# TensorE's main loop: one block per turn instead of two, its head placed on a fetch-block boundary

## The reference, cut to what matters

```python
xn = layernorm(x)
# branch 1: a state-space layer, chunked
z, xs, B, C, dt = split(xn @ in_proj_w)              # 1024, 1024, 64, 64, 16 columns
xs = silu(causal_conv1d(xs, conv_w, conv_b))         # 4 taps
B, C = elu(B) + 1, elu(C) + 1
a = exp(-softplus(dt + dt_bias) * exp(A_log))
y = ssd_chunked(C, B, xs, a) + D * xs                # 16 heads of 64, state 64 x 64
y = rmsnorm(y) * norm_scale * silu(z)
out1 = y @ out_proj_w
# branch 2: a gated feed-forward layer, with Hadamard transforms around its weights
u = hadamard(xn * SU_ug)
h = silu(u @ W_gate.T * s_gate) * (u @ W_up.T * s_up)
out2 = hadamard(h * SU_dp) @ W_down.T * s_down
return x + out1 + out2
```

## Time and profile before

| | |
|---|---|
| time, median of 3 runs | 1880.8 us (1873.93 to 1884.12) |
| profiled execution: span from first to last instruction | 1883.3 us |
| profiled execution: time around the span | not given; its span lies inside the range of the three times |
| PE busy | 1808.6 us, 96% of the span |
| PE weight loads | 1244.5 us, 66% |
| DVE, ACT, POOL busy | 74%, 65%, 16% |
| chain that ended last | PE 80%, DVE 10%, "issue" 3% |
| instruction fetches on queue q8 | 129 packets, 2.11 MB |

### The profile page before, as it was taken

One profiled execution on the slowest core, in us unless ns is written; L12 is line 12 of the kernel. 1 busy time (PEld: TensorE's weight loads), 2 busy tenths in 40 slices (PEclk: granted clock), 3 DMA queues, 4 the chain that ended last, 5 costly groups with the idle time before them and its releaser, 6 DMA issues.

```text
span 1883.3 us, 40159 instructions
## 1 busy us (share of the span) xinstructions
PE 1808.6 (96%) x13745; PEld 1244.5 (66%) x13746; DVE 1387.9 (74%) x2859; ACT 1228.6 (65%) x2583; POOL 308.9 (16%) x270
## 2 busy tenths in 40 slices
PE   5779999999999999999999999999999999999998
PEld 2346767576776767576766768677675757666674
DVE  6986867768585877758585877858686786848686
ACT  7957848476665848566574848556583857658483
POOL 0000202112030202103030211203020211203020
PEclk9989999999999999999999999999999999999999
DMA  8212122221312222121312222121312312131222
GB/s 320 71 65 57 47 57 80 46 71 34 79 43 75 62 57 79 32 71 44 81 46 58 79 46 74 37 72 46 88 49 57 79 32 82 34 80 46 61 75 57
DMA packets 217544, 125.60 MB, mean 67 GB/s; under 512 B 179662, under 2 KB 180790, under 8 KB 216886
## 3 DMA queue, kind: packets, MB, share of 16 engines
q1 hardware_dynamic: 216870, 122.30, 24.0%
q10 hardware_dynamic: 528, 1.05, 0.2%
HBM read 72.18 MB, written 8.65 MB: 43 GB/s over the span
## 4 chain that ended last, share of the span: by engine, by line
PE 80%; DVE 10%; issue 3%; DVEq 2%; SPq 2%; ACT 1%; DMA 1%; ACTq 0%
PE bank L912 78%; SPq L873 1%; DVE pair L228 1%; DVE pair L230 1%; DVEq L1287 1%; DVE wi L666 1%; DVEq L1312 1%; DVE v L1289 1%; DVE Mx L1271 1%; DVE wug L624 1%; PE bank L728 0%; PE bank L732 0%; DMA wi<-n_L_attn_out_proj_w_dram 0%; PE bank L729 0%; DVE pair L223 0%
## 5 line engine op out<-in xcount | busy, mean ns | idle before, releaser
L912 PE MATMUL bank<-pair,wug 128*128 128x256 f16 x6144 | 699.8, 273 | 0.0
L912 PEld LDWEIGHTS bank<-pair,wug 128*128 128x128 f16 x6144 | 596.3, 98 | 90.3 <-issue 3.4
L912 PE MATMUL bank<-wd,h 128*128 128x512 f16 x1536 | 360.4, 379 | 1.8 <-DVE h L1244 1.6
L1186 POOL TENSOR_TENSOR state<-state,dec 128x512 f32<-128x512 f32 x64 | 80.0, 1260 | 1104.1 <-ACT neg L1101 830.7
L1233 DVE SCALAR_TENSOR_TENSOR pair<-pair,conv 128x256 f32<-128x256 f32 x384 | 180.1, 513 | 105.5 <-ACT pair L1049 94.8
L912 PEld LDWEIGHTS bank<-wd,h 128*128 128x128 f16 x1536 | 148.0, 98 | 165.4 <-DVE h L1244 5.1
L912 PE MATMUL bank<-wi,pair 128*128 128x512 f16 (+1 forms) x1152 | 200.3, 328 | 3.6 <-DVEq L1346 3.0
L912 PE MATMUL bank<-pair,wi 128*128 128x256 f16 x1536 | 183.8, 282 | 18.9 <-issue 18.9
L912 PEld LDWEIGHTS bank<-pair,wi 128*128 128x128 f16 x1536 | 154.7, 101 | 41.9 <-issue 20.1
L1115 ACT ACTIVATE Mx<-Mx,cs_own 128x128 f32<-128x128 f32 x512 | 162.2, 387 | 6.3 <-DMA Mx<-cs_rows 5.9
L912 PEld LDWEIGHTS bank<-wi,pair 128*128 128x128 f16 x1152 | 99.6, 98 | 100.0 <-DVEq L1346 3.8
(11 more groups left out here) (253 smaller groups left out, 2716.0 us busy)
## 6 DMA issues: line engine op xcount, KB each, us to landing
Mx<-cs_rows SPq DMA_DIRECT2D x128, 256.0 KB, 3.6
pair<-in_L_attn_u_dram SPq DMA_DIRECT2D x17, 512.0 KB, 3.3
Mx<-in_L_attn_u_dram SPq DMA_DIRECT2D x16, 512.0 KB, 3.6
out_dram<-Mx SPq DMA_DIRECT2D x16, 512.0 KB, 2.8
big<-in_L_ffn_W_down_dram SPq DMA_DIRECT2D x2, 2048.0 KB, 16.8
wug<-in_L_attn_in_proj_w_dram SPq DMA_DIRECT2D x2, 2048.0 KB, 12.6
pair<-in_L_ffn_W_gate_dram SPq DMA_DIRECT2D x4, 1024.0 KB, 5.3
pair<-in_L_ffn_W_up_dram SPq DMA_DIRECT2D x3, 1024.0 KB, 15.5
```

The lines of the kernel that those rows point to most:

```text
L912: ins = nc.tensor.matmul(out, lhsT, rhs, start=first and n == 0, stop=last and n == len(pairs) - 1)
L1186: pool.tensor_tensor(half, half, bcast(dec3[:, 2, c, 8 * hf:8 * hf + 8], HD), ALU.mult).then_inc(state_faded, 1)
```

## The change

```diff
@@ -1007,9 +1007,8 @@
                                  first=False, last=not down_closes(c)).then_inc(acc_filled, 1)
 
             pe.sem_inc(ring_filled, NR)
-            with pe.Fori(0, NBLOCKS // 2) as j:
-                body(j * 2)
-                body(j * 2 + 1)
+            with nc.Fori(0, NBLOCKS, engines=[mybir.EngineType.PE], head_slot={mybir.EngineType.PE: 0}) as j:
+                body(j)
```

## The result

| | before | after |
|---|---|---|
| median | 1880.59 us (6 runs, 1873.93 to 1886.48) | 1851.2 us (6 runs, 1850.45 to 1851.78) |
| ratio | | 0.984, 95% interval 0.9821 to 0.9859 |
| span of the profiled execution | 1883.3 us | 1849.2 us (its own time: 1851.15) |
| PE's loop, first to last weight load | 1712.9 us | 1681.4 us |

The kernel is 1.6% faster, and its times now lie within 1.3 us where they were spread over 12.6. The forecast was 1852.0 (1846 to 1862).

The account below looks back on a forecast made before the run. PE's main loop was taken to bound the kernel. Its back-edge costs, 18.9 + 9.0 + 2.8 = 30.7 us, came off the 1883.3 us span to give 1852.6, taken as 1852, range 1846 to 1862.

Parts of the forecast that it names:

- PE's loop sets the time: PE is busy 96% of the span, so time taken from its main loop comes off the total nearly one for one.
- The three terms, 18.9 + 9.0 + 2.8 = 30.7 us: At PE's seven back-edges: 18.9 us of "issue" waits, 9.0 of clock drops and 2.8 of late block starts, 30.7 us together.
- The 9.0 us of the clock: In PE's loop of the kernel before, six drops of the clock were worth 9.0 us and would be gone.
- the late heads: Late block starts at PE's seven back-edges, from the branch's uncovered end: 0.4 us each, 2.8 us in all.
- The stall's cause, the distance to the block's end: PE stalls 25 matmuls behind the loop's head at a fetch-block boundary; 256 instructions behind the head would leave no stall.
- Keeping needs 8 blocks, 7 and the one ahead: PE's instruction memory holds the body's 7 fetch blocks and the one ahead, so back-edges fetch nothing: the full 30.7 us.
- Rival B: PE drops the head's block and all 15 edges fetch, hidden but for late block starts, 6.0 us: 1858.6; chance 0.13.
- Rival C: The stall belongs to PE's taken branch, not the block boundary: 15 edges at 4.4 us each, 1916 us; chance 0.07.
- Rival D: Fetches go, but each block's head waits about 2 us for xnT or O1, 30 in all: 1882.6; chance 0.04.
- A's upper end: Main case, PE keeps the loop's blocks over back-edges: 1846 to 1856 us, the upper end 1856; chance 0.76.
- a missed entry: At the loop's entry, the branch over the padding misses its target: 2.5 us more, once; taken as 0.

Follow-up runs that it names:

- slot 56: Changed kernel (one block per turn) with the loop's head placed on slot 56 of a fetch block instead of 0: 1850.13 us, ratio 0.9825.
- slot 64: Changed kernel (one block per turn) with the loop's head placed on slot 64 of a fetch block instead of 0: 1861.31 us, ratio 0.988.
- two blocks, slot 0: Kernel before, still two blocks per turn, with the loop's head placed on slot 0 of a fetch block: 1852.25 us, ratio 0.985.
- slots 64 and 96: Changed kernel with only the head's slot moved from 0 to 64 or 96: 1861.31 us, ratio 0.988, and 1861.21 us, ratio 0.99.
- slot 160: Kernel before, two blocks per turn, with the head placed on slot 160, 96 instructions from its block's end: 1855.83 us, ratio 0.9858.
- slot 200: Kernel before, two blocks per turn, with the head placed on slot 200, 56 instructions from its block's end: 1879.04 us, ratio 0.9998.
- slot 224: Kernel before, two blocks per turn, with the head placed on slot 224, 32 instructions from its block's end: 1882.5 us, ratio 1.0016.

## Why the prediction was right

*PE's loop sets the time.* Right: PE's loop became 31.5 us shorter, the total 29.4.

*The three terms, 18.9 + 9.0 + 2.8 = 30.7 us.* The sum held. The 9.0 us of the clock can be read in the trace of before. Over the 3.40 us behind the first stall 32 matmuls ran at a granted clock of 1.00, behind the second and the last 18 and 19 at 0.55 and 0.58, and behind the four between them:

```profile
806.89:810.29 3.40, 3.40 (x17) 0.50 0.43 159
1021.62:1025.02 3.40, 3.40 (x18) 0.54 0.43 159
1236.74:1240.14 3.40, 3.40 (x18) 0.53 0.32 117
1451.50:1454.90 3.40, 3.40 (x19) 0.57 0.43 159
```

That is 83 matmuls fewer in six stretches, 8.8 us at 0.106. In the changed kernel all three terms are gone: the "issue" waits, the drops of the clock but the one at the entry, and the late heads (the gap before a block's first weight load is 0.12 us at each of the 15 edges, where it was 0.33 to 0.77 at the seven of before). By length of the blocks, 16 x 105.15 - 0.2 = 1682.2 was forecast and 1681.4 measured, inside of which the first block has a drop of the clock that the forecast left out. The span came out 3.4 us below the forecast one, 1.8 of it because PE's loop began at 161.7 instead of 163.5, in a preparation stage that the change doesn't touch. The profiled execution's time is 2.0 above its span, which took most of that back in the predicted time. So the closeness of 1852.0 and 1851.2 is in part luck.

*The stall's cause, the distance to the block's end.* Right, and now shown by the slots: it lies where the boundary lies.

*Keeping needs 8 blocks, 7 and the one ahead.* Right, and shown by 56 against 64. The trace of before could not show it. ACT and DVE, with loops of 278 and 290 instructions, showed that a body that fits is kept, but not that seven blocks and one fit on PE; that part was a bet. The changed kernel goes round 15 times over seven blocks with 10 packets in all, and so does slot 56; with an eighth block of the body (slot 64) it is 146.

*What was mis-weighed.* The prediction hung the full gain on keeping: "The change is worth the full 30.7 us if PE holds 8 blocks". The runs say that the placed head gives about 28 of the 29 us without keeping anything (two blocks, slot 0), and that one body without a placed head gives nothing. The two work together only in that a placed head makes seven blocks of what would be eight.

*Rival B*, nothing kept but hidden, was priced at 6.0 us over the forecast. The kernels that are in that case (slots 64 and 96) are 10 over the changed kernel. The term that was missing is DVE, late for D12 at 15 blocks, 6.0 us. And the late head is not the branch's uncovered end, as I had put it ahead of the transposes: with a branch of 0.36 us (the two-block loop with the hint) the heads are as late (0.36 to 0.84 us of idle) as with one of 3.6 (the two-block loop on slot 0, 0.34 to 0.84), and they start right behind the landing. The size was right, 0.4 us an edge: the seven gaps of the kernel before are 0.52 us in the mean, where 0.12 is usual. Its source was wrong.

*Rival C*, the stall belongs to the branch, fell with slots 0 and 160. Its price was taken from the kernel before, 4.4 us an edge; the one-block loop that really stalls 15 times pays 2.2. The stall is not a constant of the edge: it went from 1.2 to 3.8 us over these kernels, and the drop of the clock behind it came with some and not with others. From the block's first matmul to the one behind the stall it is 4.3 to 4.7 us in the kernel before, 3.0 to 4.1 in the unplaced one-block loop, 3.2 to 4.3 on slot 200 and 3.7 to 4.9 on slot 224. So the second block can come sooner in a two-block loop too; why is open, and it was not tried.

*Rival D*, the gain goes into new waits: 0.2 us of them in sixteen blocks on end.

*Two slips that change nothing.* A's upper end was set at 1856, while its own terms, 1855 and a missed entry of 2.5, make 1857.5. And nine blocks of the kernel before have no stall, not eight; seven of them lie behind one with a stall.

Also open is how a fetch delays a transpose. The traces show them at the same time and the transpose longer, which is no proof of what they share. How DVE becomes late for D12 is open as well.

## What to carry to other kernels

Where an engine that sets the time stands still for "issue" a fixed number of instructions behind a loop's head, count its instructions in fetch blocks: look at where the head lies in its block first, since moving it by one argument gave here what halving the loop alone did not. Then see whether the body and the one block fetched ahead fit in what the engine keeps (eight blocks of 256 instructions on PE here: 10 packets with them, 146 with a ninth); if it is over by one, the back-edge hint or another slot may bring it in (145 packets to 9, and 146 to 10). And look for the price of fetches in small transfers beside them (a transpose takes up to 2.5 us on slot 64, 1.27 in the changed kernel) and in the waits on other engines (6.0 us for DVE there), not in the engine's own waits for code alone. It depends on when the fetches fall: here 122 packets cost 1 us and 146 cost 10.

## What the runs showed of the hardware that was not expected

- The back-edge hint saved one packet a turn in the two-block loop (15 instead of 16) and turned 145 packets into 9 in the one-block loop.
- In the profiled executions the granted clock fell once in fifteen behind PE stalls of 1.2 to 2.3 us (the unplaced one-block loop), five times in seven behind the 2.0 us stalls of slot 200, six in seven behind the 2.7 us stalls of before, and seven in seven behind the 3.1 us stalls of slot 224. The length of the stall alone doesn't tell which (2.34 us without a drop, above; 1.96 us with one at slot 200).
- PE's wait of 3.0 to 3.1 us for DVE at the loop's entry is in all fourteen profiles. The clock fell behind it in ten (0.51 to 0.69 over the next 3.40 us) and not in four (before, slots 56 and 96 of the one-block loop, slot 160 of the two-block loop). This alone moves a time by 1.6 us or so, with no change in the program.
- The times of the kernels that stall spread over 9 to 13 us (1874.38 to 1886.61 for slot 200, in ten runs), those of the kernels that don't over 1 to 4.4, in four to six runs each.
